# Two statistics passes and the scores in one place of TensorE's order, from slot 20 on

## The chip, the cores and the metric

The kernel runs on one core of a Trainium2 chip. The metric is the device time of one execution in microseconds (us). A profiled execution gives, beside its time, a trace with every instruction of every engine. TensorE does the matmuls, VectorE and ScalarE the elementwise work, GpSimd further elementwise work, and SyncE (SP) issues most of the DMAs; ScalarE issues others.

## What is computed

The input x has 64 sequences of 64 tokens with 512 features. A per-sequence 64 x 64 matrix mixes the tokens' features first (the condition), and then a block of 16 heads with 128 columns each follows. Reduced to what matters here:

```
q = layernorm(silu(conv4(h @ Wq)))          # per head, over its 128 columns
k = layernorm(silu(conv4(h @ Wk)))
v = h @ Wv;  beta = sigmoid(h @ Wb + bb);  gate = silu(h @ Wg)
S = (1 - beta_t) S + beta_t * outer(v_t, k_t);  o_t = S q_t      # scan over the tokens
x = x + (o * gate) @ Wo
h2 = x @ W2.T + adapter(x)
x = x + ternary_ffn(h2)                      # rows quantized to 8 bit, weights to -1, 0, 1
```

The recurrence is computed for each sequence as (scores of k and q, weighted by products of the decays) times v. All large products are made in three passes of a split into a high and a low part.

## The kernel before

The 4096 tokens are cut into 8 groups of 512. One head of one group is a **unit** (128 units), and the program runs in **slots**, one for each unit, with five more at the end. The slot U belongs to head U mod 16 of group U div 16. Each engine has a program of its own, a loop over the slots, and what an engine does in a slot stands in the order in which it is written; the engines meet in semaphores alone. TensorE's loop is at the end of the function (lines 1381 to 1399). In slot U it does this, in order:

- the projection of q for unit U (12 matmuls with 512 columns, line 1325, helper at 1147), into the bank pj_a;
- in even slots the **means** pass (line 1334): for the two units U-2 and U-1 the sums over the 128 columns of q and k, as matmuls with 32 columns of weights, four strips side by side, into the bank `stat`;
- the projection of k for unit U, into pj_b;
- in odd slots the **variance** pass (line 1343), strips of the same shape, of the squares of the two units U-3 and U-2;
- the slot's first tiles (`make(U, 0)`), by a table written out by hand (`SLOT_TILES`): tiles of v, of the output product o, and in some heads the work of the second half (transpositions x2 and xqt, the adapter xa, the dense product h, the ternary product f). They go into a ring of four banks;
- the **scores** of unit U-4 (line 1354): 16 small matmuls with 64 columns of weights, into one bank;
- the projection of the gate g for unit U, again into pj_a, the slot's second tiles, and the product of the weighted scores with v for unit U-4 (line 1364, "pv").

Between the strip passes of a pair of units lies a chain over the other engines. ScalarE copies the means from the bank (`keep_means`, line 1011); a DMA writes four rows of them to memory and two more bring them back spread over all partitions (from slot ROWS_SP = 20 on SP issues these, lines 357 to 366, before it on ScalarE's queue). VectorE subtracts the means from q (`centre_q`, line 837) and GpSimd from k (line 548), and ScalarE makes the squares (line 1005). After the variance pass ScalarE and VectorE make the reciprocal deviations (lines 1059 and 841 to 846), which go the same way through memory (r_rows, lines 368 to 375). In the next even slot VectorE multiplies both units with them (`normalise`, line 853) and GpSimd applies weight and bias (`affine`, line 559): q and k of unit U-4 first, those of U-3 behind them. The scores of a unit wait for its affine. SP's queue also carries, behind `send_means` of an even slot, that slot's loads of the weights of v, o and W2.

VectorE in a slot: the scan of the decays, in even slots `normalise`, the taps of the convolution for q and k, in odd slots the Newton step, its part of the first tiles (`take(U, 0)`), the weighing of the scores of unit U-4 (`weigh`, line 864), in even slots `centre_q`, its part of the second tiles, and the gating of the output (line 871).

Of the kernel before, what the change touches and what calls it, by code (L numbers as in the profile page):

```python
# [101 lines left out]
def adaln_attn_ffn(nc, x, subjects, adapters, cond_w, Wq, Wk, Wv, Wb, bb, Wg, Wo, qconv_w, qconv_b,  # L102
# [12 lines left out]
    UNITS = GROUPS * H  # L115
# [6 lines left out]
    ROWS_SP = H + 4  # L122
# [14 lines left out]
    with ExitStack() as ctx:  # L137
# [101 lines left out]
        def ring_bank(kind, n, t):  # L239
            return ring[ring_no[kind, n, t] % TILE_RING]  # L240

        def made(kind, n, t=0):

            no = ring_no[kind, n, t]
            return S[f"ring_mm{no % TILE_RING}"], no // TILE_RING + 1
# [9 lines left out]
        def taken_sem(kind, n, t=0):  # L255
            return taken(kind, n, t)[0]
# [343 lines left out]
        def _(dve):  # L600
# [181 lines left out]
            def take(U, at):  # L782
                for kind, n, t in tiles_at(U, at):
                    if kind == "cond":
                        cond_lo(n, t)
                    elif kind == "ad":
                        adapter_scales()
                    elif kind in ("sa", "sb", "sw"):
                        split_setup(kind, t)
                    elif kind == "gam":  # L790
                        ternary()
                    elif kind == "gr":
                        dve.wait_ge(*made("gr", 0))
                        V.tensor_copy(gamma_cols, ring_bank("gr", 0, 0)[0:KC, 0:P]).then_inc(taken_sem("gr", 0), 1)
                    elif kind == "st":
                        keep_ternary(t)
                    elif kind == "z":
                        keep_row(n)
                    elif kind == "bt":
                        beta_columns(n)  # L800
                    elif kind == "v":
                        scale_v(n, t)
                    elif kind == "o":
                        accumulate(n, t)
                    elif kind == "x2":
                        x2_low(n, t)
                    elif kind == "xa":
                        adapt(n, t)
                    elif kind == "small":
                        row_scales(n, t)  # L810
                    elif kind == "quant":
                        quantize(n, t)
                    elif kind == "f":
                        scale_out(n, t)
# [24 lines left out]
            def newton(m):  # L839
                dve.wait_ge(S["seed"], m + 1)  # L840
                V.scalar_tensor_tensor(out=stat[:], in0=stat[:], scalar=LN_EPS, in1=rstd[:], op0=ALU.add, op1=ALU.mult
                                       ).then_inc(S["newton_a"], 1)
                dve.wait_ge(S["newton_a"], m + 1)
                V.tensor_tensor(stat[:], stat[:], rstd[:], ALU.mult).then_inc(S["newton_b"], 1)
                dve.wait_ge(S["newton_b"], m + 1)
                V.scalar_tensor_tensor(out=rstd[:], in0=stat[:], scalar=3.0, in1=rstd[:], op0=ALU.subtract, op1=ALU.mult
                                       ).then_inc(S["rr"], 1)
# [39 lines left out]
            for U in range(SLOTS):  # L887
                if 0 <= U - 4 < UNITS:
                    scan(U - 4)
                if U % 2 == 0 and 4 <= U <= UNITS + 2:  # L890
                    normalise(U - 4)
                    normalise(U - 3)
                if U < UNITS:
                    taps("q", U)
                    taps("k", U)
                if U % 2 and 3 <= U <= UNITS + 1:
                    newton((U - 3) // 2)
                take(U, 0)
                if 0 <= U - 4 < UNITS:
                    weigh(U - 4)  # L900
                if U % 2 == 0 and 2 <= U <= UNITS:
                    centre_q(U - 2)
                    centre_q(U - 1)
                take(U, 1)
                if 0 <= U - 4 < UNITS:
                    gate_out(U - 4)

        @block.scalar
        def _(act):
# [103 lines left out]
            def send_means(m):  # L1013
                act.wait_ge(S["mean_kept"], m + 1)
                for u in range(2 if m else 0):
                    act.wait_ge(S[f"m_in{u}"], 16 * m)
                act.dma_start(m_rows, rstd[0:P:32, :]).then_inc(S["m_out"], 16)
# [19 lines left out]
            def load_head(name, u):  # L1037
                act.wait_ge(S[f"proj_{name}"], u)
                if u == H:
                    act.wait_ge(S[f"saved_{name}"], 16 * H)  # L1040
                act.dma_start(block_both(name, u % H), parts[name][u % H]).then_inc(S[f"w{name}_in"], 16)
# [49 lines left out]
            for U in range(SLOTS):  # L1091
                blocks = split_blocks(U) if U < H + 3 else []
                if 0 <= U - 5 < UNITS:
                    gated_hi(U - 5)
                if U < UNITS:
                    first_tap("q", U)
                if H <= U + 1 < UNITS:
                    load_head("q", U + 1)
                if U % 2 == 0 and 2 <= U <= UNITS:
                    keep_means(U // 2 - 1)  # L1100
                    if U < ROWS_SP:
                        send_means(U // 2 - 1)
                for b in blocks:
                    if b[0] == "q":
                        split_hi(b)
                if U < UNITS:
                    first_tap("k", U)
                if H <= U + 1 < UNITS:
                    load_head("k", U + 1)
                if U % 2 and 3 <= U <= UNITS + 1:  # L1110
                    seed((U - 3) // 2)
                if U < UNITS:
                    silu("q", U)
                    silu("k", U)
                if U % 2 == 0 and 2 <= U < ROWS_SP:
                    spread_means(U // 2 - 1)
                if U % 2 and 3 <= U < ROWS_SP:
                    send_rstd((U - 3) // 2)
                take(U, 0)
                for b in blocks:  # L1120
                    if b[0] == "k":
                        split_hi(b)
                if U < UNITS:
                    gate(U)
                if H <= U + 1 < UNITS:
                    load_head("g", U + 1)
                if U % 2 and 3 <= U < ROWS_SP:
                    spread_rstd((U - 3) // 2)
                for b in blocks:
                    if b[0] in "vog":  # L1130
                        split_hi(b)
                if U % 2 == 0 and 2 <= U <= UNITS:
                    for u in (U - 2, U - 1):
                        squares("q", u)
                        squares("k", u)
                take(U, 1)

        @block.tensor
        def _(pe):
# [188 lines left out]
            def means(m):  # L1328
                pe.wait_ge(S["silu_q"], 2 * m + 2)
                pe.wait_ge(S["silu_k"], 2 * m + 2)  # L1330
                if m:
                    pe.wait_ge(S["rr"], m)
                for j in range(4):
                    mm = T.matmul(stat[32 * j:32 * j + 32, :], mean[:], y["qk"[j % 2]][:, (2 * m + j // 2) % Y_RING, :],
                                  start=True, stop=True)
                mm.then_inc(S["mean_made"], 1)

            def variance(m):
                pe.wait_ge(S["sq_q"], 2 * m + 2)
                pe.wait_ge(S["sq_k"], 2 * m + 2)  # L1340
                pe.wait_ge(S["mean_kept"], m + 1)
                for j in range(4):
                    mm = T.matmul(stat[32 * j:32 * j + 32, :], mean[:], sq["qk"[j % 2]][:, j // 2, :], start=True, stop=True)
                mm.then_inc(S["var"], 1)
# [36 lines left out]
            for U in range(SLOTS):  # L1381
                if U < UNITS:
                    project("q", U)
                if U == 0:
                    turn_tables()
                if U % 2 == 0 and 2 <= U <= UNITS:
                    means(U // 2 - 1)
                if U < UNITS:
                    project("k", U)
                if U % 2 and 3 <= U <= UNITS + 1:  # L1390
                    variance((U - 3) // 2)
                make(U, 0)
                if 0 <= U - 4 < UNITS:
                    score(U - 4)
                if U < UNITS:
                    project("g", U)
                make(U, 1)
                if 0 <= U - 4 < UNITS:
                    attend(U - 4)
# [27 lines left out]
```

## Time and profile before

| what | value |
|---|---|
| median of 3 runs | 2485.77 us |
| lowest and highest | 2485.18 and 2485.89 us |
| the profiled execution | 2486.88 us |
| its span, first to last instruction | 2485.1 us |
| TensorE busy | 2397.0 us, 96% |
| VectorE busy | 1656.6 us, 67% |
| ScalarE busy | 1073.3 us, 43% |
| GpSimd busy | 817.4 us, 33% |
| moved by DMA | 551.21 MB |

"Busy" is the share of the span in which an engine has an instruction running. TensorE's matmuls are pipelined, so the step from the start of one to the start of the next says more than the duration of one. Waits are idle time of an engine ahead of an instruction, put down to what released it.

### The profile page before, as it was taken

Reading aid. Unit: us, or ns where it says so; the run is one execution under the profiler, and the core shown is the slowest. Engines: PE = TensorE matmul, PEld = TensorE weight load, DVE = VectorE, ACT = ScalarE, POOL = GpSimd, SP = SyncE. Lnnn points to the kernel's source line nnn. Section 1 sums busy time; section 2 is a strip of 40 time slices with the busy share of each in tenths; the row PEclk is TensorE's granted clock in tenths of the full one; section 3 lists DMA queues with packets and bytes.
Section 4 is the critical chain, followed back from the end, with each engine's and each line's share of the span. In section 5 each row is a group of like instructions: output and inputs, shape, how many; then the busy total and the mean of one; then the engine's idle time right before and its main releaser. Section 6 shows DMA issues by size and latency. Waiting matters only on the chain. (4 is left out here: it accounts for less than half of the span.)

```text
span 2485.1 us, 36012 instructions
## 1 busy us (share of the span) xinstructions
PE 2397.0 (96%) x13268; PEld 1837.6 (74%) x13268; DVE 1656.6 (67%) x2653; ACT 1073.3 (43%) x1615; POOL 817.4 (33%) x637
## 2 busy tenths in 40 slices
PE   6789999999999999999999999999999999999986
PEld 5567777777777777777777777777777777777765
DVE  4656666776667666676666766667666776667763
ACT  4545544443444444453444443443443543444431
POOL 3466543232233223323133232333133222333330
PEclk9999999999999999999999999999999999999997
DMA  6788867566666666668566585656766566666650
GB/s 219 244 311 296 292 227 262 185 233 220 219 227 217 228 217 227 201 201 278 184 225 228 179 279 188 226 203 207 260 219 233 191 236 213 220 231 208 227 195 17
DMA packets 290088, 551.21 MB, mean 222 GB/s; under 512 B 94259, under 2 KB 118875, under 8 KB 289915
## 3 DMA queue, kind: packets, MB, share of 16 engines
q1 hardware_dynamic: 235714, 353.55, 42.4%
q10 hardware_dynamic: 54200, 195.36, 23.3%
q8 instruction: 107, 1.75, 0.3%
q14 instruction: 67, 0.54, 0.1%
HBM read 495.08 MB, written 53.74 MB: 221 GB/s over the span
## 5 line engine op out<-in xcount | busy, mean ns | idle before, releaser
L552 POOL TENSOR_TENSOR og_lo<-gt,og_hi 128x512 fp32r<-128x512 f32 x128 | 179.2, 1400 | 1136.8 <-ACT og_hi L1071 1136.8
L830 DVE SCALAR_TENSOR_TENSOR y_q<-pj_a,conv,y_q 128x504 f32<-128x504 f32 (+2 forms) x384 | 281.1, 732 | 125.8 <-ACT y_q L1048 116.2
L1147 PE MATMUL pj_a<-ht_hi,wg 128*128 128x512 f32 x1024 | 356.3, 409 | 5.8 <-DVE y_q L830 5.5
L1147 PE MATMUL pj_a<-ht_hi,wq 128*128 128x512 f32 x1024 | 348.9, 402 | 8.0 <-issue 4.0
L1147 PE MATMUL pj_b<-ht_hi,wk 128*128 128x512 f32 x1024 | 344.5, 397 | 0.0
L1147 PE MATMUL ring<-wv,ht_hi 128*128 128x512 f32 x1024 | 319.6, 393 | 0.5 <-POOL wv L542 0.5
L548 POOL TENSOR_TENSOR y_k<-y_k,sq_both 128x512 f32<-128x512 f32 x128 | 205.2, 1609 | 342.2 <-DMA sq_both<-m_rows 342.0
L830 DVE SCALAR_TENSOR_TENSOR y_k<-pj_b,conv,y_k 128x504 f32<-128x504 f32 (+2 forms) x384 | 281.4, 733 | 52.3 <-ACT y_k L1048 43.2
L1147 PE MATMUL ring<-wo,og_hi 128*128 128x512 f32 x992 | 312.5, 396 | 0.0
L1147 PEld LDWEIGHTS pj_b<-ht_hi,wk 128*128 128x128 f32 x1024 | 192.1, 188 | 91.8 <-issue 49.5
L1147 PEld LDWEIGHTS pj_a<-ht_hi,wg 128*128 128x128 f32 x1024 | 195.5, 191 | 53.4 <-issue 4.0
L1147 PEld LDWEIGHTS ring<-wv,ht_hi 128*128 128x128 f32 x1024 | 189.7, 188 | 59.9 <-issue 21.0
L1147 PEld LDWEIGHTS ring<-wo,og_hi 128*128 128x128 f32 x992 | 183.8, 188 | 64.2 <-issue 26.0
L1147 PEld LDWEIGHTS pj_a<-ht_hi,wq 128*128 128x128 f32 x1024 | 192.6, 188 | 47.1 <-issue 7.0
L1065 ACT ACTIVATE gt<-pj_a 128x512 f32<-128x512 f32 x128 | 76.4, 597 | 332.1 <-PE pj_a L1147 330.0
L1071 ACT ACTIVATE og_hi<-gt 128x512 fp32r<-128x512 f32 x128 | 80.7, 630 | 302.1 <-DVE gt L871 302.1
L1147 PE MATMUL pj_a<-ht_lo,wg 128*128 128x512 f32 x512 | 203.2, 397 | 0.0
L1147 PE MATMUL pj_a<-ht_lo,wq 128*128 128x512 f32 x512 | 199.9, 390 | 0.0
L1147 PE MATMUL ring<-wv,ht_lo 128*128 128x512 f32 x512 | 199.5, 390 | 0.0
L1147 PE MATMUL pj_b<-ht_lo,wk 128*128 128x512 f32 x512 | 199.4, 390 | 0.0
L1147 PE MATMUL ring<-wo,og_lo 128*128 128x512 f32 x496 | 193.5, 390 | 0.0
L559 POOL TENSOR_SCALAR y_q<-y_q,ln_q 128x512 f32<-128x512 f32 x128 | 185.4, 1449 | 24.5 <-DVE y_q L853 24.5
(194 smaller groups left out, 4150.1 us busy)
## 6 DMA issues: line engine op xcount, KB each, us to landing
wq<-parts_q ACTq DMA_DIRECT2D x112, 512.0 KB, 3.7
wk<-parts_k ACTq DMA_DIRECT2D x112, 512.0 KB, 5.5
wg<-parts_g ACTq DMA_DIRECT2D x112, 512.0 KB, 6.5
wv<-parts_v SPq DMA_DIRECT2D x112, 512.0 KB, 8.9
sq_both<-m_rows SPq DMA_DIRECT2D x110, 512.0 KB, 5.9
sq_both<-r_rows SPq DMA_DIRECT2D x110, 512.0 KB, 5.2
wo<-parts_o SPq DMA_DIRECT2D x108, 512.0 KB, 8.7
keep<-keep_rows SPq DMA_DIRECT2D x256, 64.0 KB, 6.0
```

What stands on the lines that cost most here:

```text
L548: G.tensor_tensor(c, c, sq["k"][:, u % 2, :], ALU.subtract).then_inc(S["c_k"], 1)
L552: G.tensor_tensor(og_lo[:, u % OG_RING, :], gt[:, u % GT_RING, :], og_hi[:, u % OG_RING, :].bitcast(F32), ALU.subtract).then_inc(S["oglo"], 1)
L559: G.tensor_scalar(c, c, ln[x_][:, 2:3], ln[x_][:, 1:2], ALU.mult, ALU.add).then_inc(S[f"aff_{x_}"], 1)
L830: V.scalar_tensor_tensor(out=yy[:, :, k:], in0=pp[:, :, :L - k], scalar=conv[:, i, h, 3 - k:4 - k], in1=yy[:, :, k:], op0=ALU.mult, op1=AL ...
L1065: A.activation(gt[:, u % GT_RING, :], pj["g"][:], ACT.Silu).then_inc(S["gated"], 1)
L1071: A.activation(og_hi[:, u % OG_RING, :], gt[:, u % GT_RING, :], ACT.Identity).then_inc(S["oghi"], 1)
L1147: last = T.matmul(psum, a, b, start=start and n == 0 and m == 0, stop=stop and n == len(pairs) - 1 and m == 2)
```

## The change

From slot 20 (ROWS_SP) on:

- TensorE: the means pass of an even slot stands behind the projection of k, where the variance pass of an odd slot stands already, and the scores of unit U-4 follow right behind, ahead of the slot's first tiles.
- VectorE: the weighing of unit U-4 stands ahead of its part of the first tiles.
- ScalarE: in even slots the copy of the means stands behind the first tap of k and the load of the next head's k weights. (The copy in slots below 20 and its DMA there stay as they were.)

Nothing is added or left out. SP's, GpSimd's and the DMAs' programs are the same.

```diff
@@ VectorE's loop
                 if U % 2 and 3 <= U <= UNITS + 1:
                     newton((U - 3) // 2)
+                if ROWS_SP <= U < UNITS + 4:
+                    weigh(U - 4)
                 take(U, 0)
-                if 0 <= U - 4 < UNITS:
+                if 4 <= U < ROWS_SP:
                     weigh(U - 4)
@@ ScalarE's loop
-                if U % 2 == 0 and 2 <= U <= UNITS:
+                if U % 2 == 0 and 2 <= U < ROWS_SP:
                     keep_means(U // 2 - 1)
-                    if U < ROWS_SP:
-                        send_means(U // 2 - 1)
+                    send_means(U // 2 - 1)
...
                 if H <= U + 1 < UNITS:
                     load_head("k", U + 1)
+                if U % 2 == 0 and ROWS_SP <= U <= UNITS:
+                    keep_means(U // 2 - 1)
@@ TensorE's loop
-                if U % 2 == 0 and 2 <= U <= UNITS:
+                if U % 2 == 0 and 2 <= U < ROWS_SP:
                     means(U // 2 - 1)
                 if U < UNITS:
                     project("k", U)
                 if U % 2 and 3 <= U <= UNITS + 1:
                     variance((U - 3) // 2)
+                elif U % 2 == 0 and ROWS_SP <= U <= UNITS:
+                    means(U // 2 - 1)
+                if ROWS_SP <= U < UNITS + 4:
+                    score(U - 4)
                 make(U, 0)
-                if 0 <= U - 4 < UNITS:
+                if 4 <= U < ROWS_SP:
                     score(U - 4)
```

## Rows read from the trace of the kernel before

**Rows 1.** The page: engines' busy time, and granted clock in 40 slices.
```profile
PE 2397.0 (96%) x13268; PEld 1837.6 (74%) x13268; DVE 1656.6 (67%) x2653; ACT 1073.3 (43%) x1615; POOL 817.4 (33%) x637
...
PEclk9999999999999999999999999999999999999997
```

**Rows 2.** TensorE's waits: instruction, releaser, us in total, times, longest.
```profile
PE m L1354 <- POOL y_q L559: 8.2, 3, 4.2
```

**Rows 3.** Timeline (start us, length us), slot 67: last matmuls of k and g.
```profile
1263.13 0.39 PE L1147 MATMUL pj_b<-ht_hi,wk 128*128 128x512 f32 x1
...
1270.64 0.39 PE L1147 MATMUL pj_a<-ht_hi,wg 128*128 128x512 f32 x1
```

**Rows 4.** Timeline, slot 127 (no first tiles): k's last, scores, g's last.
```profile
2375.38 0.39 PE L1147 MATMUL pj_b<-ht_hi,wk 128*128 128x512 f32 x1
...
2376.69 0.69 PE L1354 MATMUL m<-y_q,y_k 128*64 128x64 f32 x16
...
2379.93 0.39 PE L1147 MATMUL pj_a<-ht_hi,wg 128*128 128x512 f32 x1
```

**Rows 5.** Timeline, slot 66: last of q, of k and of tile v; affine of k.
```profile
1243.84 0.39 PE L1147 MATMUL pj_a<-ht_hi,wq 128*128 128x512 f32 x1
...
1247.79 0.39 PE L1147 MATMUL pj_b<-ht_hi,wk 128*128 128x512 f32 x1
...
1250.51 0.39 PE L1147 MATMUL ring<-wv,ht_lo 128*128 128x512 f32 x1
...
1246.77 0.77 POOL L559 TENSOR_SCALAR y_k<-y_k,ln_k 128x512 f32<-128x512 f32 x1
```

**Rows 6.** Timeline, slot 56 (head 8): last of q, affine of k.
```profile
1048.64 0.39 PE L1147 MATMUL pj_a<-ht_hi,wq 128*128 128x512 f32 x1
...
1052.63 0.77 POOL L559 TENSOR_SCALAR y_k<-y_k,ln_k 128x512 f32<-128x512 f32 x1
```

**Rows 7.** Timeline, slot 58 (head 10): q's last, affine, scores, two waits behind.
```profile
1087.32 0.39 PE L1147 MATMUL pj_a<-ht_hi,wq 128*128 128x512 f32 x1
...
1094.36 0.77 POOL L559 TENSOR_SCALAR y_k<-y_k,ln_k 128x512 f32<-128x512 f32 x1
...
1095.23 0.69 PE L1354 MATMUL m<-y_q,y_k 128*64 128x64 f32 x16
...
1102.94 0.40 PE L1245 MATMUL ring<-ident_bf,xq 128*128 128x128 bf16 x4 [0.75 <-DVE xq L768]
1103.72 1.16 PE L1364 MATMUL ring<-decay_bd,v 128*128 128x128 f32 x8 [0.38 <-DVE decay_bd L864]
```

**Rows 8.** Slot 78 (head 14), and busy time, clock, DMA share, GB/s ahead.
```profile
1462.28 0.39 PE L1147 MATMUL pj_a<-ht_hi,wq 128*128 128x512 f32 x1
...
1466.72 1.72 POOL L559 TENSOR_SCALAR y_k<-y_k,ln_k 128x512 f32<-128x512 f32 x1
...
1434.00:1456.00 22.00, 22.00 (x129) 16.90 (x129) 14.60 (x23) 10.44 (x16) 4.54 (x4) 1.00 1.03 355
```

**Rows 9.** Timeline, slots 128 to 130: scores, variance pass, scores, pv.
```profile
2390.71 0.69 PE L1354 MATMUL m<-y_q,y_k 128*64 128x64 f32 x16 [1.05 <-issue]
...
2398.94 1.07 PE L1343 MATMUL stat<-sq_both,mean 128*32 128x512 f32 x8
...
2414.90 0.69 PE L1354 MATMUL m<-y_q,y_k 128*64 128x64 f32 x16 [0.98 <-POOL y_q L559]
2416.55 1.16 PE L1364 MATMUL ring<-decay_bd,v 128*128 128x128 f32 x8 [0.97 <-DVE decay_bd L864]
```

**Rows 10.** Scores that waited ahead of slot 20, g's last, and one stretch.
```profile
172.59 1.12 PE L1354 MATMUL m<-y_q,y_k 128*64 128x64 f32 x16 [4.18 <-POOL y_q L559]
...
178.49 0.40 PE L1147 MATMUL pj_a<-ht_hi,wg 128*128 128x512 f32 x1
...
171.60:178.40 6.80, 5.81 (x27) 4.76 (x28) 4.64 (x8) 1.89 (x3) 4.62 (x6) 0.50 0.91 303
...
244.67 0.69 PE L1354 MATMUL m<-y_q,y_k 128*64 128x64 f32 x16 [3.01 <-POOL y_q L559]
```

## The prediction

> **What bounds the kernel now.** I read the page first: TensorE is busy in 2397.0 of 2485.1 us, and from the fourth slice of 40 on nearly without a gap, at its full granted clock until the last slice [rows 1]. So the time is the sum of what TensorE does, and an edit pays only if it shortens TensorE's own stream, and costs only where it makes TensorE wait. The list of TensorE's waits comes next: the scores wait three times for GpSimd's affine of q, 8.2 us in all [rows 2]; two of these waits lie ahead of slot 20 and one at the end [rows 10, 9]. In the steady part, which the change touches, no score waits. The third view is the timeline of single slots. Whether the scores still do not wait when they stand earlier is the whole question, so for each head I compare when GpSimd ends the affine of that unit's k with when TensorE would reach the scores in the new order.
>
> **Gain: one change of shape fewer in each slot.** In an ordinary odd slot the last matmul of k starts at 1263.13 and the last of g at 1270.64 [rows 3]: 7.51 us for the strip pass, one tile, the scores and g. Slot 127 has no first tiles, so there the scores already follow the strip pass: from the last of k, 2375.38, to the last of g, 2379.93, are 4.55 us [rows 4]. A tile of 12 matmuls without a change of shape ahead of it takes 1250.51 less 1247.79, 2.72 us [rows 5]. New order: 4.55 + 2.72 = 7.27, a gain of 0.24 a slot. An even slot gains as much, since its pass leaves the place between q and k for the same place. Slots 20 to 126 are 107; the 7 of head 10 are counted below, so 100 x 0.24 = **-24 us**. If shapes changed for nothing the gain would be 0; that is its other end.
>
> The Trainium skill, TensorEngine Tiling (Array Packing), Key Properties, says that changing the tiling mode drains TensorE, by which 32 columns to 64 is a change too. The 4.55 us of slot 127 hold that change, so its price is in the gain already. By that rule alone only the count of changes falls, and the sum would end at -24.
>
> **Where the scores fall due.** In the new order k follows q (2.72), and the scores start 1.31 behind k's last matmul (2376.69 less 2375.38 [rows 4]): 4.03 behind the last start of q. What must be done by then is the affine of k of unit U-4, which in an even slot GpSimd makes in that very slot; for an odd slot it is made a slot before, so odd slots only gain.
> - Ordinary even slot: due 1243.84 + 4.03 = 1247.87; the affine ends at 1246.77 + 0.77 = 1247.54 [rows 5]. 0.33 us of room, and a score that waited follows its affine by 0.1 (1095.23 against 1095.13 [rows 7]). No wait, but the room is small: of heads 0, 2, 4, 6 and 12 some 33 slots hang on it. **+4 us**, between 0 and 8 (a quarter of a us each).
> - Head 8: due 1048.64 + 4.03 = 1052.67, affine ends 1053.40 [rows 6]: a wait of 0.73 and the 0.1. Seven slots: **+6 us**.
> - Head 10: due 1087.32 + 4.03 = 1091.35, affine ends 1095.13, the scores already stand at 1095.23 [rows 7]. The scores cannot move forward at all, while the tile of v and the one of f, which fill this time today, come behind them: 1095.23 less 1091.35, less the 0.24 of the shape, 3.65 us. VectorE, late since the row scales of slot 9, no longer holds up the transposition of xq (0.75) and the weighing (0.38) [rows 7], so 1.1 of it comes back: 2.5 a slot, seven slots: **+18 us**. VectorE's lateness starts from TensorE's own f tile in slot 9, so it moves along with TensorE and does not heal.
> - Head 14: in slot 78 due 1462.28 + 4.03 = 1466.31, affine ends 1468.44 [rows 8], a wait of 2.2; in other groups the transfer of the reciprocal deviations comes in time. Here the moved pass matters: mean copy, transfer of the means, and on SP's queue behind it the loads of wo and then of wv all go up to 2.7 us later (one projection). In the 22 us ahead of slot 78's transfer the DMA engines are full (share 1.03 [rows 8]), so the backlog that r_rows stands behind ends up to 2.7 later. Between 0 and 4.9 a slot; I take 2.5, the middle. Seven slots: **+17.5 us**.
>
> **The moved pass elsewhere.** ScalarE's copy now stands behind the first tap of k, so means reach VectorE and GpSimd some 2.7 us later and the squares end later; their reader, the strip pass of the next odd slot, stands a whole k projection behind that slot's q. I cost this at nothing; if that cover is gone, it comes back in the 0 to 8 above. SP's other loads behind the means (heads 0, 2, 4, 6) have a slot or more until they are read. VectorE waits at the weighing for scores that are long done (its taps of k end later); the tiles' release moves behind one weighing, and four banks take that up.
>
> **The end.** In slot 128 the scores stand at 2390.71, behind two tiles of v, and could not go earlier for the affine. In the new order these two tiles come behind them, 2 x 2.72 = 5.4; the variance pass goes from 2398.94 to 2404.3. From it the chain variance, deviations, transfer, affine leads to the scores of unit 126, 15.96 later today (2414.90), so 2420.3; there two tiles of o now come behind the scores too, and the product with v, at 2416.55 today, comes at 2420.3 + 0.7 + 5.4 = 2426.4 [rows 9]. **+10 us**, on no one's cover.
>
> **The clock.** After a wait of 4.18 us at 172.59 the granted clock stood at 0.50, its lower level of 1.2 GHz: scores to last of g took 5.90 us (172.59 to 178.49) instead of 3.24 in slot 127. After 3.01 us at 244.67 it stayed at the full 2.4 GHz [rows 10, 4, 1]. The new waits of head 10 (3.9) lie between, nearer the first; those at the end, 5.4 and the idle time of about 1 that stands ahead of these scores today [rows 9], are longer; head 14's are mostly shorter. I take 5 of 7, 2 of 2 and 2 to 3 of 7: 9.5 x 2.66 = **+25 us**, between 5 (the end alone) and 43. The Trainium skill, TensorE: Matmul & The Clock Gate, What's actually happening, calls the lower clock the default that activity lifts; the first row agrees.
>
> **Sum.** -24 + 4 + 6 + 18 + 17.5 + 10 + 25 = +56.5. The profiled execution took 2486.88 us with a span of 2485.1; the median of the runs is 2485.77. I add the sum to the median: **2542 us**.
>
> **Rivals.**
> 1. The waits come, but the clock holds and the queue's shift hides in other traffic: -24 + 6 + 18 + 10 with head 14 between 0 and 15 and the end's drop at most: +10 to +30, about 2508. For it: the 3.01 us wait left the clock alone. Against: the waits of head 10 are longer.
> 2. Faster: the affines come as early as the scores, because VectorE, weighing sooner, is ahead everywhere. Then only the changes of shape count, and the two waits of head 10 vanish with them: -24 - 1.7 - 7 x 1.1 = -33, 2452. It decides at head 10: the affine there must end 3.9 us earlier. Against it: what makes it late starts from TensorE's tile of f, not from the weighing.
> 3. The change does not do what it says: scores behind 32-column strips drain as long as before in all, gain 0, waits as forecast: +80, 2566.
> 4. Waits of heads 8 and 10 cost about what the shapes give, the rest nothing: within 5 us of before.
>
> The Trainium skill, TensorE: Matmul & The Clock Gate, The mechanism, has matmuls start and end strictly in order, which speaks against putting a wait ahead of tiles that are ready. The scores at 172.59, with g behind them, agree [rows 10].
>
> **Chances.** Forecast 0.59, rival 1 0.26, rival 2 0.06, rival 3 0.05, rival 4 0.04. 0.2% of the time, 5 us, is about what a measurement can tell here. Faster 0.06, same 0.04, slower 0.90. The range takes in the forecast with its bounds and most of rival 1: 2503 to 2564.
>
> **What would show it.** Right: in the list of waits, scores held by GpSimd's affine some 16 to 25 times after slot 20, in heads 8, 10, 14 and at the end; a granted clock below full in the middle slices; k's last to g's last 7.27 in odd slots. Wrong: no such waits (rival 2), waits with a full clock (rival 1), 7.5 us in odd slots (rival 3). Waits in heads 0 to 6 by more than 0.3 us would mean that the later means pull the whole chain along, and the time could pass the range.

## The result, and the profile after

The changed kernel takes **2520.49 us** (median of 4 runs, 2517.82 to 2528.64) against 2485.47 for the kernel before (4 runs, 2484.11 to 2485.89): ratio 1.0142, 95% interval 1.0129 to 1.0154. It is 35 us slower. The forecast was 2542 in a range of 2503 to 2564.

The profiled execution of the changed kernel took 2523.17 us with a span of 2521.4, 36.3 more than the span before; the shares below are worked out from these two spans. In the changed code the lines of TensorE's helpers stand three lower: L1357 are the scores, L1367 the product with v, L1346 the variance pass, L1248 the transposition of xq. VectorE's and GpSimd's lines are those of before. The page first, TensorE's row and its granted clock in 40 slices, as in [rows 1]:

```profile
PE 2393.5 (95%) x13246; PEld 1862.2 (74%) x13268; DVE 1680.1 (67%) x2653; ACT 1078.1 (43%) x1615; POOL 815.4 (32%) x637
...
PEclk9999999999999999999999999999999999999987
```

TensorE's busy time has hardly changed (2397.0 before), and the span is 36 longer: TensorE now waits. The page's clock row shows nothing of what follows; its slices are 63 us long, and the drops are a few us each. TensorE's waits say what it waits for (instruction, releaser, us in all, times, longest), to be held against [rows 2]:

```profile
PE m L1357 <- issue: 36.4, 18, 6.9
PE m L1357 <- POOL y_q L559: 24.8, 7, 3.8
...
PE ring L1248 <- DVE xq L768: 9.4, 8, 5.8
...
PE ring L1367 <- DVE decay_bd L864: 5.2, 3, 2.0
```

The same list of the kernel before has two more rows on the scores beside the one of [rows 2], the only one that the forecast named:

```profile
PE m L1354 <- POOL y_k L559: 7.7, 1, 7.7
PE m L1354 <- issue: 3.7, 2, 2.6
```

So beside one wait of some 7 us near the start, which both kernels have, the scores waited five times, 11.9 us in all: three times ahead of slot 20, and twice by about 1 us at the end. Now they wait 25 times, 61.2 us in all. The profile puts 18 of these waits down to "issue", but there too GpSimd's affine of k ends 0.1 ahead of the scores (at 2415.02 and 2445.32 in the two longest, scores at 2415.12 and 2445.42). From slot 20 on there are 22 of them, 51.8 us: one of 1.87 in slot 20, seven of 0.77 in head 8, seven of 3.38 to 3.79 in head 10, five of 0.26 to 2.10 in head 14, and two of 6.49 and 6.89 in slots 128 and 130.

What the change was meant to bring is there as well. Slot 67, an odd one, on the timeline (start, length):

```profile
1274.14 0.39 PE L1150 MATMUL pj_b<-ht_hi,wk 128*128 128x512 f32 x1
1275.46 0.69 PE L1357 MATMUL m<-y_q,y_k 128*64 128x64 f32 x16
...
1281.41 0.39 PE L1150 MATMUL pj_a<-ht_hi,wg 128*128 128x512 f32 x1
```

From the last start of k to the last of g are 7.27 us, where [rows 3] gave 7.51. That is the 7.27 of the forecast to the digit. (A change of shape is a step of TensorE from matmuls with 128 columns of weights to some with 64 or 32, or back.)

Slot 58 of head 10 is the other side. TensorE's q, means and scores, the last of g and the next slot's q; GpSimd's affine; the transposition of xq:

```profile
1088.58 0.47 PE L1150 MATMUL pj_a<-ht_hi,wq 128*128 128x512 f32 x1
...
1091.20 0.39 PE L1150 MATMUL pj_a<-ht_hi,wq 128*128 128x512 f32 x1
...
1094.69 0.59 PE L1337 MATMUL stat<-y_q,mean 128*32 128x512 f32 x1
...
1098.22 0.77 POOL L559 TENSOR_SCALAR y_k<-y_k,ln_k 128x512 f32<-128x512 f32 x1
...
1099.09 1.12 PE L1357 MATMUL m<-y_q,y_k 128*64 128x64 f32 x16 [3.79 <-POOL y_q L559]
...
1108.32 0.39 PE L1150 MATMUL pj_a<-ht_hi,wg 128*128 128x512 f32 x1
...
1112.11 0.40 PE L1248 MATMUL ring<-ident_bf,xq 128*128 128x128 bf16 x4 [0.45 <-DVE xq L768]
...
1113.21 0.47 PE L1150 MATMUL pj_a<-ht_hi,wq 128*128 128x512 f32 x1
```

The affine ends at 1098.99 and the scores follow 0.1 later. They take 1.12 instead of the 0.69 of slot 67: the clock has fallen. The granted clock of this stretch, and of two stretches that hold the waits of slots 128 and 130 (stretch, its length, PE, PEld, DVE, ACT, POOL busy, then the granted clock, DMA share, GB/s):

```profile
1097.00:1104.50 7.50, 5.41 (x27) 4.42 (x28) 5.73 (x10) 1.53 (x3) 3.50 (x4) 0.54 0.83 311
...
2412.00:2419.00 7.00, 3.88 (x24) 3.24 (x25) 3.21 (x6) 0.00 (x0) 5.80 (x6) 0.54 0.60 182
2442.00:2449.00 7.00, 3.58 (x22) 3.01 (x23) 3.54 (x6) 0.00 (x0) 4.34 (x4) 0.52 0.10 26
```

0.5 is 1.2 GHz: in each of the three the clock stood at the lower level nearly all the time. The first 2.1, 3.1 and 3.4 us of them are still the wait itself; the rest is work at the lower clock. Over the whole span the granted clock is 0.977, where it was 0.988.

**Where the 36.3 us of the two spans lie.** I measured each slot from its first q to the first q of the next, in both traces, and took the difference. The forecast's terms stand beside it, regrouped by slot (they were rounded there, and add up to 56.8 here):

| stretch | forecast | measured |
|---|---|---|
| heads other than 8, 10, 14 in slots 21 to 126 | -16.6 (-20.6 shapes, +4 waits) | -19.0 (-0.23 in nearly every slot) |
| slot 20, once | in the row above | +3.3 |
| head 8, seven slots | +4.3 | +4.2 |
| head 10, seven slots | +31.3 (18 waits, 13.3 clock) | +29.5 |
| head 14, seven slots | +22.5 (15.8 waits less shapes, 6.7 clock) | +8.5 |
| slot 127 to the end | +15.3 (10 waits, 5.3 clock) | +11.6 |
| ahead of slot 20, which the change doesn't touch | 0 | -1.8 |

### The profile page after: what moved, and what is told of

It reads as the page before. It is cut to its first block and busy times, and to the rows that moved or that the text cites. A ratio compares the mean times of both kernels' runs of the same rounds, so it can differ in the third digit from the quotient of the medians.

```text
span 2521.4 us, 35990 instructions
## 1 busy us (share of the span) xinstructions
PE 2393.5 (95%) x13246; PEld 1862.2 (74%) x13268; DVE 1680.1 (67%) x2653; ACT 1078.1 (43%) x1615; POOL 815.4 (32%) x637
## 3 DMA queue, kind: packets, MB, share of 16 engines
q8 instruction: 107, 1.75, 0.3%
## 5 line engine op out<-in xcount | busy, mean ns | idle before, releaser
L1150 PE MATMUL pj_a<-ht_hi,wg 128*128 128x512 f32 x1024 | 347.2, 400 | 5.2 <-DVE y_q L830 5.2
L1150 PE MATMUL pj_b<-ht_hi,wk 128*128 128x512 f32 x1024 | 337.4, 390 | 0.0
L1150 PE MATMUL ring<-wv,ht_hi 128*128 128x512 f32 x1024 | 332.3, 406 | 0.7 <-POOL wv L542 0.7
L1150 PE MATMUL ring<-wo,og_hi 128*128 128x512 f32 x992 | 318.5, 402 | 0.4 <-DMA wo<-parts_o 0.4
L707 DVE TENSOR_TENSOR acc<-acc,ring 128x512 f32<-128x512 f32 x128 | 87.7, 687 | 171.8 <-PE ring L1150 170.3
L1357 PEld LDWEIGHTS m<-y_q,y_k 128*64 128x64 f32 x2048 | 73.9, 142 | 167.1 <-issue 111.0
```

Of the source, the lines that this page charges most:

```text
L707: V.tensor_tensor(a, a, ring_bank("o", s, t)[:], ALU.add).then_inc(taken_sem("o", s, t), 1)
L1150: last = T.matmul(psum, a, b, start=start and n == 0 and m == 0, stop=stop and n == len(pairs) - 1 and m == 2)
L1357: mm = T.matmul(m0[at:at + L, b // 2 * L:(b // 2 + 1) * L], ck[:, cols], cq[:, cols], start=True, stop=True)
```

## Experiments

In all of these the place of each step is given by two conditions: `front(U)`, the slots in which scores and weighing stand ahead of the first tiles, and `late(U)`, the even slots in which means pass and copy stand behind k. In the changed kernel `front` is ROWS_SP <= U < UNITS + 4 and `late` is ROWS_SP <= U <= UNITS in even slots. In their code GpSimd's and VectorE's lines stand seven lower than in the changed kernel, and TensorE's eight.

### Which part costs: the late means, or the early scores

The means pass and its copy moved alone:

```diff
 def front(U):
-    return ROWS_SP <= U < UNITS + 4
+    return False
```

> Only the means pass and its copy move behind k (even slots from 20 on); scores and weighing stay where they were before. Theory A (the loss comes from scores that reach TensorE ahead of their affine): the number of changes of shape in a slot is as before and no score is early, so 2486 us, within 4 of before. Theory B (the loss comes from means that start a projection later and pull transfers and loads behind them): 10 to 35 us slower than before, 2496 to 2521.

Measured: 2487.59 us (10 runs, 2485.2 to 2491.01) against 2486.69 before, ratio 1.0005, 0.9996 to 1.0015. Nearly every slot is within 0.05 us of before, all seven of head 14 among them; two slots each of heads 10 and 13 differ by 0.3 to 0.9. The late means by themselves cost and bring nothing: with the scores where they were, nobody waits for what comes later.

The scores and the weighing alone, in the odd slots alone:

```diff
 def front(U):
-    return ROWS_SP <= U < UNITS + 4
+    return ROWS_SP <= U < UNITS + 4 and U % 2 == 1
 def late(U):
-    return U % 2 == 0 and ROWS_SP <= U <= UNITS
+    return False
```

> Scores and weighing ahead of the tiles in odd slots alone; even slots as before. Theory A: the affine of an odd slot's unit is made a slot earlier, so nothing waits, and 53 slots gain 0.23 each: 12 us faster, 2473. Theory C (weighing ahead of VectorE's part of the tiles, or scores right behind the strips, cost something by themselves): no gain, 2486 or more.

Measured: 2474.39 us (2473.59 to 2475.81), ratio 0.9949, 0.9932 to 0.9966. From slot 21 to 126 nearly every odd slot is 0.23 shorter (slot 75 is 0.37 longer), and the even ones stay as they were within 0.02, but for three of head 10 that differ by 0.3. The gain is real, and odd slots have no wait, as the forecast said. It comes with one change of shape fewer: the means pass moved alone, with as many changes as before, gained nothing. What makes up the 0.23 inside TensorE is not shown.

### The same where the affine comes in time

```diff
 def front(U):
-    return ROWS_SP <= U < UNITS + 4
+    return ROWS_SP < U < UNITS and U % H not in (8, 10, 14)
 def late(U):
-    return U % 2 == 0 and ROWS_SP <= U <= UNITS
+    return U % 2 == 0 and ROWS_SP < U < UNITS and U % H not in (8, 10, 14)
```

> The change in slots 21 to 127 without heads 8, 10 and 14, and not in slots 128 to 131; there the order of before. Theory A: 85 slots gain 0.23, no score waits: 19 us faster, 2466. Theory B: the later means of heads 0, 2, 4, 6 and 12 still cost, the sum is at or above 2486.

Measured: **2466.55 us** (4 runs, 2465.84 to 2467.48) against 2486.69, ratio 0.992, 0.9903 to 0.9936. It is the fastest version of this study, 20 us below the kernel before and 54 below the changed one. Its scores wait five times beside the one near the start, as in the kernel before, where the changed kernel's wait 25 times; three of the five lie ahead of slot 20, two of 0.82 and 0.98 at the end:

```profile
PE m L1365 <- POOL y_k L566: 7.0, 1, 7.0
PE m L1365 <- issue: 5.2, 2, 4.3
PE m L1365 <- POOL y_q L566: 3.4, 3, 1.6
```

Heads 8, 10 and 14 show +0.0, +0.2 and +0.0 us in all, the other 85 slots from 21 to 126 -0.23 almost throughout. So the changed kernel's loss lies in heads 8, 10 and 14, slot 20 and the end, and nowhere else.

### Head 10, and the end, put back

```diff
 def front(U):
-    return ROWS_SP <= U < UNITS + 4
+    return ROWS_SP <= U < UNITS + 4 and not (U < UNITS and U % H == 10)
 def late(U):
-    return U % 2 == 0 and ROWS_SP <= U <= UNITS
+    return U % 2 == 0 and ROWS_SP <= U <= UNITS and U % H != 10
```

> The changed kernel with the order of before in head 10's seven slots. Theory A: their waits and the lower clock behind them go, 7 x 4.2 plus 0.2 each: 29 to 31 us off the changed kernel, 2490. If waits only moved on to a later place (theory D), less than 10 us are gained, 2510 or more.

Measured: 2491.0 us (10 runs, 2487.91 to 2498.23), ratio 1.0015, 1.0005 to 1.0025. 29.5 less than the changed kernel (30.7, if each is held against the kernel before of its own series), about as much as its seven slots of head 10 had added in the profile.

```diff
 def front(U):
-    return ROWS_SP <= U < UNITS + 4
+    return ROWS_SP <= U < UNITS
 def late(U):
-    return U % 2 == 0 and ROWS_SP <= U <= UNITS
+    return U % 2 == 0 and ROWS_SP <= U < UNITS
```

> The changed kernel with the order of before from slot 128 on. Theory A: the tiles stand ahead of the scores again at the end, so the 11 to 12 us that the end lost come back: 2508 to 2510. Theory D (the end only carries on what was late earlier): within 4 of the changed kernel, 2517 to 2524.

Measured: 2506.19 us (4 runs, 2503.42 to 2515.49), ratio 1.0093, 1.0067 to 1.0119. From slot 127 to the end its profile is 0.5 longer than before, the changed one 11.6: the new order of the end costs 11.1. The median is 14.3 below the changed kernel's, more than theory A expected; in its profile head 10 adds 25.2 instead of 29.5, slot 20 adds 0.8 instead of 3.3 and head 14 6.4 instead of 8.5, as the clock falls less often there. These vary from run to run.

### Head 10: the wait or the clock

Twelve matmuls that nobody reads, into the bank that the next tile clears anyway, while the scores wait:

```diff
@@ TensorE's loop, ahead of the scores
+if ROWS_SP <= U < UNITS and U % H == 10:
+    first = tiles_at(U, 0)[0]
+    free_bank(*first)
+    for _ in range(12):
+        T.matmul(ring_bank(*first)[:], ht_hi[:, 0, 0:P], ht_hi[:, 1, :], start=True, stop=True)
```

> The changed kernel; in head 10's seven slots TensorE makes 12 matmuls with 512 columns that nobody reads (into the bank of the next tile, which starts anew) between the means pass and the waiting scores. They need about 3.3 us of a wait of 3.5. Theory A1 (of the 4.2 us that a slot of head 10 lost, 2.7 are the wait and 1.5 the lower clock behind it): the clock stays up in head 10, 7 x 1.5 = 10 us off, 2510. Theory A2 (the wait is all of it, the lower clock costs nothing): no gain, 2520 or a little more.

Measured: 2505.52 us (4 runs, 2500.48 to 2505.89), ratio 1.0073, 1.0055 to 1.009: 15 us less than the changed kernel, by adding work. Its slot 58, and the granted clock around the scores:

```profile
1087.23 0.47 PE L1158 MATMUL pj_a<-ht_hi,wq 128*128 128x512 f32 x1
...
1093.89 3.02 PE L1409 MATMUL ring<-ht_hi 128*128 128x512 f32 x12
1097.45 0.69 PE L1365 MATMUL m<-y_q,y_k 128*64 128x64 f32 x16 [0.54 <-issue]
...
1104.36 0.39 PE L1158 MATMUL pj_a<-ht_hi,wg 128*128 128x512 f32 x1
...
1107.31 0.62 PE L1256 MATMUL ring<-ident_bf,xq 128*128 128x128 bf16 x8
...
1108.63 0.47 PE L1158 MATMUL pj_a<-ht_hi,wq 128*128 128x512 f32 x1
...
1096.00:1103.50 7.50, 6.96 (x45) 5.03 (x44) 7.24 (x13) 1.26 (x2) 2.86 (x4) 1.00 0.82 305
```

The scores take 0.69 again, and from them to the last of g are 6.91 us, where the changed kernel has 9.23 (1099.09 to 1108.32). The slot takes 21.40 instead of 24.63. The wait for xq is gone as well.

The matmuls change more than the clock, so this alone could mislead. The kernel with the old end has the control: two of its seven slots of head 10 kept the full clock by themselves, with the wait unfilled. Slot 42 of it:

```profile
790.14 0.47 PE L1158 MATMUL pj_a<-ht_hi,wq 128*128 128x512 f32 x1
...
800.37 0.69 PE L1365 MATMUL m<-y_q,y_k 128*64 128x64 f32 x16 [3.50 <-POOL y_q L566]
...
811.54 0.47 PE L1158 MATMUL pj_a<-ht_hi,wq 128*128 128x512 f32 x1
...
796.00:803.50 7.50, 4.00 (x35) 2.66 (x28) 7.36 (x11) 3.51 (x6) 5.77 (x5) 1.00 1.01 373
```

A wait of 3.50 with the clock at 1.00: the slot takes 21.40 too. So the wait costs a slot of head 10 the same with and without filling: 1.75 to 1.77 more than before in six of the seven filled slots, 1.77 and 1.73 in the two unfilled ones. What the changed kernel has beyond that, 3.89 to 4.95 less 1.77, comes with the lower clock: 2.1 to 3.2 us a slot, 17.1 in seven. By the granted clock from the scores on, about 13.7 of it are lost to the clock itself (a stretch at 0.5 loses half its length). Most of the rest is the wait for xq, 0.45 to 0.56 a slot. Over four kernels it is there in 24 of the 25 unfilled slots of head 10 whose clock fell, and gone in the three that kept it.

### The weighing's place

```diff
@@ VectorE's loop
-if ROWS_SP <= U < UNITS + 4:
-    weigh(U - 4)
 take(U, 0)
-if 4 <= U < ROWS_SP:
+if 4 <= U < UNITS + 4:
     weigh(U - 4)
```

> The changed kernel with VectorE's weighing behind its part of the first tiles, as before. Theory A (the weighing's place is not what counts): within 3 of the changed kernel, 2517 to 2524. Theory C (weighing ahead of the tiles holds VectorE up, and with it the normalising behind): 5 us or more faster.

Measured: 2527.63 us (4 runs, 2519.83 to 2534.08), ratio 1.0166, 1.0137 to 1.0196. That is above theory A's range too, but the interval overlaps that of the changed kernel (1.0129 to 1.0154). It is not faster, so the early weighing is not what costs; whether it helps by some us is not shown. In its one slot of head 10 with the clock held (slot 90, a wait of 3.49) the slot is 1.75 longer than before, as with the early weighing: there the place makes no difference.

### Head 14: does the moved pass push the transfer back

The forecast had head 14's wait grow because the means of head 12 come up to 2.7 us later and the transfer of the reciprocal deviations stands behind them. First in the changed kernel, then in the version "where it fits" with head 14 added:

```diff
@@ in the changed kernel
 def late(U):
-    return U % 2 == 0 and ROWS_SP <= U <= UNITS
+    return U % 2 == 0 and ROWS_SP <= U <= UNITS and U % H != 12
```

> The changed kernel with the means pass and its copy between q and k, as before, in head 12's seven slots; scores ahead of the tiles everywhere as in the change. It gives up 0.23 in these slots. Theory B14 (head 14's waits come from head 12's loads starting a projection later): the waits of head 14 shrink from about 1 to 0.5 us each, and 2 to 8 us are gained, 2512 to 2518. Theory A14 (head 14's transfer is as late without that): 1 to 2 us lost, 2522.

Measured: 2525.88 us (2524.98 to 2526.45), ratio 1.0161, 1.0144 to 1.0178. Not faster, and above the figures of both theories. Head 14 adds 5.1 in its profile (8.5 in the changed kernel); there its clock held, where it fell twice in the changed kernel, and the waits by themselves add up to 6.7 instead of 7.0.

```diff
@@ in the version where it fits
 def front(U):
-    return ROWS_SP < U < UNITS and U % H not in (8, 10, 14)
+    return ROWS_SP < U < UNITS and U % H not in (8, 10)
 def late(U):
-    return U % 2 == 0 and ROWS_SP < U < UNITS and U % H not in (8, 10, 14)
+    return U % 2 == 0 and ROWS_SP < U < UNITS and U % H not in (8, 10)
```

> The version with the change only where it fits (2466.55 us), with head 14 given the new order as well: head 14's term by itself, without head 10's waits and without the new end. By the forecast's term (2.5 us a slot less 0.24 for the shape, seven slots) the time is 2466.55 + 15.8 = 2482.4, and more if the clock falls. By what the changed kernel showed in head 14 (sum +8.5 with two low-clock stretches, +6.55 in the run with filled waits) it is 2473 to 2476.

Measured: 2473.35 us (4 runs, 2470.95 to 2474.71) against 2488.35 before, ratio 0.9938, 0.9921 to 0.9954. Head 14 adds 4.7 in the profile. The forecast's 2.5 a slot falls.

```diff
@@ in the kernel just above
 def late(U):
-    return U % 2 == 0 and ROWS_SP < U < UNITS and U % H not in (8, 10)
+    return U % 2 == 0 and ROWS_SP < U < UNITS and U % H not in (8, 10, 12)
```

> The same with head 12's means pass and its copy left between q and k, so that in head 12 only the scores and the weighing move. If the later means of head 12 push the transfer that head 14's affine waits for (the forecast's queue shift, up to 2.7 us a slot), this is 4 us or more below the version with all of head 14 and head 12 moved. If that transfer is late anyway, the two lie within 2 us, this one up to 1.7 us higher where the change of shape comes back in head 12 (7 x 0.24).

Measured: 2475.24 us (2474.16 to 2480.28), ratio 0.9952, 0.9935 to 0.9968: 1.9 above the one before it, not 4 below. Head 14 adds 9.0 here, two of its slots with 3.6 each from a fallen clock. The waits of head 14's scores add up to 7.5 here and to 6.3 in the one before. In the two kernels with head 12's means early they are 6.7 and 7.5, in the six with early scores in head 14 and head 12's means late 6.3 to 9.2. A queue shift that is worth 4 us is not there.

A smaller one may be read from the traces. VectorE's multiplication in head 14 waits for the transfer; slot 62 of the changed kernel, the last of q, the multiplication and the scores:

```profile
1172.84 0.39 PE L1150 MATMUL pj_a<-ht_hi,wq 128*128 128x512 f32 x1
...
1175.20 0.69 DVE L853 TENSOR_TENSOR y_q<-y_q,sq_both 128x512 f32<-128x512 f32 x1 [3.39 <-DMA sq_both<-r_rows]
...
1179.04 0.85 PE L1357 MATMUL m<-y_q,y_k 128*64 128x64 f32 x16 [2.10 <-issue]
```

Here it starts 2.36 behind the last start of q. The mean of that over the seven slots is 0.66, 0.86, 1.10 and 1.20 in the four kernels in which head 12's means stand where they did (before, the odd slots alone, and the two with head 12 early), and 1.27 to 1.59 in the eight in which they stand behind k. So the late means go with a transfer that is later by about half a us in the mean (0.3 among the kernels with early scores in head 14, 0.7 among the others), and not by the 2.7 of a projection. This is one execution of each kernel, and single slots lie anywhere between -0.3 and 2.8.

## Right and wrong, step by step

**The bound and the direction: right.** TensorE's stream sets the time, and scores that stand ahead of ready tiles make it wait. The list of waits shows what the forecast named: scores held by GpSimd's affine in heads 8, 10, 14 and at the end, 22 times from slot 20 on, one of them in slot 20 itself (16 to 25 were forecast). The Trainium skill, TensorE: Matmul & The Clock Gate, The mechanism, on matmuls that start strictly in order, pointed the same way, and the trace agrees: in slot 58 no matmul starts in the 3.79 us ahead of the scores, and the tile of v comes only behind them, at 1100.15.

**The gain: right.** -0.23 a slot against -0.24. Rival 3, no gain, is excluded by the odd slots' own run, and rival 4, within 5 us of before, by the 35 us.

**Ordinary even slots: +4 forecast, 0 measured.** The room of 0.33 us was enough in every one of them; from slot 21 on heads 0, 2, 4, 6 and 12 have no wait. The means' later arrival, costed at nothing, did cost nothing.

**Head 8: right.** 0.77 waited where 0.73 and 0.1 were read from [rows 6].

**Head 10: right in sum, by luck: two parts were off and met.** The wait is there as read from [rows 7]. It costs 1.77 a slot, 12.4 in all, instead of 2.5 and 18: the scores come up to 0.4 earlier in the slot than before, and with the clock held more than 1.1 comes back behind them. With the clock down, less comes back, and of the two waits that were to vanish only the one of the weighing does; xq still waits, 0.45 in slot 58. The clock made up for it: 17.1, with the wait for xq in it, instead of 13.3. It fell in all seven slots, where five were taken.

**Head 14: the step that failed.** 17.5 us were taken for the waits, the middle of 0 to 4.9 a slot. Measured from the last start of q to the scores, with 4.03 as the slot without a wait, the seven waits add up to 7.0, or 1.0 a slot. Two things were mis-sized: slot 78, on which the upper end rested, was the latest of the seven before (2.52 against a mean of 0.66), and the queue's shift is near 0.5 and not up to 2.7. The trace before had the rest as well. That "in other groups the transfer of the reciprocal deviations comes in time" was misread; in slot 30 of the kernel before the last of q and the affine of k are

```profile
568.34 0.39 PE L1147 MATMUL pj_a<-ht_hi,wq 128*128 128x512 f32 x1
...
571.17 1.73 POOL L559 TENSOR_SCALAR y_k<-y_k,ln_k 128x512 f32<-128x512 f32 x1
```

The affine ends at 572.90, where the scores would fall due at 572.37. By this measure four of head 14's seven slots were late before, by 0.53, 0.36, 2.13 and 0.48, and three in time: 3.5 us in all. Read over all seven, the term would have stood near 4, and the 7.0 measured lie 3 above that and 10 below the 17.5. The clock fell in two slots here, forecast 2 to 3, and head 14's clock cost about 3.1 (8.5 less 7.0 and with 1.6 of the shapes back). This term is most of the 20 us by which the forecast's sum, 56.5, stands above the 36.3.

**The end: nearly right.** +10 and 5.3 for the clock were forecast, 11.6 measured. The clock fell at both waits, as forecast, but cost less. From slot 127 to the end, before and after (stretch, its length, busy times, granted clock, DMA share, GB/s):

```profile
2370.05:2485.09 115.04, 86.14 (x457) 63.84 (x456) 57.65 (x109) 26.81 (x47) 24.70 (x20) 0.87 0.27 92
2394.74:2521.41 126.67, 87.54 (x456) 65.72 (x456) 56.92 (x109) 26.59 (x47) 24.07 (x20) 0.84 0.25 86
```

TensorE's idle time grows by 10.2 (28.9 to 39.1), close to the forecast's +10, and its busy time by 1.4. The granted clock goes only from 0.87 to 0.84: in the kernel before, too, it was down in parts of the end, at which the forecast did not look. The scores of slots 128 and 130 and the product that follows the second:

```profile
2415.12 1.12 PE L1357 MATMUL m<-y_q,y_k 128*64 128x64 f32 x16 [6.49 <-issue]
...
2445.42 1.12 PE L1357 MATMUL m<-y_q,y_k 128*64 128x64 f32 x16 [6.89 <-issue]
...
2453.33 1.05 PE L1367 MATMUL ring<-decay_bd,v 128*128 128x128 f32 x8
```

These two waits alone are 13.4 us, in place of about 1 us each before.

**Not foreseen: slot 20.** The first slot in the new order waited 1.87 and lost clock behind it, 3.3 us in all in this execution, once. The forecast had named a wait of more than 0.3 in heads 0 to 6 as the sign that the later means pull the chain along. It is not that here: the means of this slot's unit 16 are made in slot 18, which the change leaves alone. VectorE waited 3.25 for the reciprocal deviations there. In the five other kernels with slot 20 in the new order the wait is anything from none to 1.68, and before there were 0.03 us of room, where other slots of head 4 had 0.32. Why that transfer varies is open.

**The clock in sum:** 25 forecast; 17.1 in head 10, about 3.1 in head 14, some 1.4 at the end and a part of slot 20's 3.3, so near 23. That the sum is right is partly luck: the clock fell more often in head 10 than was taken, and cost less at the end. The test named for it, a clock below full in the page's middle slices, was a poor one: a slice is too long to show such drops.

**The rivals.** Rival 1 (2508, the clock holds) is wrong in its mechanism, but the kernel with head 10 filled shows it for the steady part: 2505.52. Rival 2 (faster) fell at its point of decision: head 10's scores came up to 0.4 earlier in the slot, not 3.9.

## What to carry to other kernels

Before an instruction moves forward on a strictly ordered engine, read for every kind of slot when its input is ready and when it would now be reached; move it only where there is room, and leave the other slots as they are: here that made +35 us into -20. A wait ahead of work that was ready costs twice on TensorE, by itself and by the clock behind it, so a wait of 2 to 4 us should be priced with what a lower clock costs on top, here 1.6 to 3.2 us. And take the size of a repeated wait from all its repetitions, not from the worst.

## What the hardware showed that was not expected

**The length of a wait alone does not decide whether the clock falls.** In the kernel before, 4.18 us lowered it and 3.01 did not [rows 10], and the forecast put the line between. But slot 62 lost its clock behind 2.10 us in the changed kernel and kept it behind 2.19 in the one with head 10 filled:

```profile
1178.00:1184.00 6.00, 4.96 (x28) 4.09 (x29) 5.34 (x9) 1.26 (x2) 2.45 (x3) 0.72 0.73 257
```

The same slot with head 10 filled, its scores and the stretch around them:

```profile
1174.00 0.69 PE L1365 MATMUL m<-y_q,y_k 128*64 128x64 f32 x16 [2.19 <-issue]
...
1173.00:1179.00 6.00, 5.00 (x35) 4.21 (x36) 5.79 (x10) 1.27 (x2) 2.41 (x3) 1.00 0.76 284
```

And of 28 waits of head 10, all between 3.38 and 3.80 us, in the changed kernel and in three unfilled variants (old end, weighing behind, head 12 early), three kept the clock. The length still counts. Between slots 20 and 126 of all kernels here, eight of nine waits of the scores between 1.87 and 2.19 us lowered the clock, and none of the 76 between 0.6 and 1.82 did. So the forecast's line, above 3 us, was too high. What decides between two equal waits is open.

**Filling a wait with unread matmuls keeps the clock**: 12 of them gave back 17.4 us over seven slots by the two profiles, and 15.0 by the medians. The Trainium skill, TensorE: Matmul & The Clock Gate, HAM oscillation — how this bites in real kernels, tells of a loop whose wait lowers the clock anew in every turn; head 10's seven slots agree, with 2.1 to 3.2 us each. It was not tried to put the filling where the other waits are; where the scores can stay behind the tiles, that is cheaper.
